# Two attentions of an eight-layer kernel: products in four pieces, maxima split on GpSimd, zero rows by DMA

## The chip, the cores and the metric

The kernel runs on one core of a Trainium2 chip. A core has TensorE (PE, matrix products into PSUM), VectorE (DVE), ScalarE (ACT), GpSimd (POOL, which reaches SBUF only) and SyncE (SP, which here issues nearly all DMAs). Each engine runs its own instructions in order and waits on semaphores for the others. The metric is the time of one execution in microseconds on the device, the median of several runs. PE's clock has two levels, 1.2 and 2.4 GHz; the profile gives the granted clock as a share of the higher one.

## What is computed

The reference is a chain of eight layers on x of 8 x 512 x 128 (float32), attention and feed-forward in turn. The change touches layers 0 and 2 of it, the two multi-head attentions with 16 heads of 8 dimensions each. In the first, two query heads share one of 8 key heads and there is no mask:

```python
scores = jnp.einsum('bsnd,btnd->bnst', q4, k4) * scale
probs = jax.nn.softmax(scores, axis=-1)
a_dot = jnp.einsum('bnst,btnd->bsnd', probs, v4)
```

In the second there are 16 key heads and a causal mask:

```python
scores = jnp.einsum('bhqd,bhkd->bhqk', q, k) / jnp.sqrt(jnp.asarray(d, q.dtype))
mask = jnp.tril(jnp.ones((T, T), dtype=bool))
scores = jnp.where(mask, scores, jnp.asarray(-jnp.inf, q.dtype))
attn = jax.nn.softmax(scores, axis=-1)
return jnp.einsum('bhqk,bhkd->bhqd', attn, v)
```

Between them and after them stand memory terms, mixtures of experts, a two-way state space layer and a last attention, which the change leaves alone.

## The kernel before

`attend` computes one attention for all eight batch rows (chunks, `b`) of 512 tokens. It is called twice, first with `a.causal` false, then with it true; `call` is 0 or 1.

Queries and keys are stacked in SBUF as bf16 parts (72 rows: three parts by three parts of 8 dimensions), `q[k]` and `kk[k]`, two buffers each, k = b mod 2. A score tile (`score_tile`, L771) is a matmul of 128 queries by up to 512 keys over rows 0 to 95 of the stacks, into one of two PSUM banks `sc`; DVE takes the maximum over keys (L911) into `top`. There are four tiles per head. In the causal case tile t covers (t + 1) x 128 keys, and a small matmul with `mask_q` (L774) adds the mask.

When four heads (a group, `g`) are through, `split` (L885 and following) writes the negated maxima as three bf16 parts into `max_part`, a chain of four short DVE instructions on 128x16. PE turns them into rows in bank 0 of `sc` (`turn`, L819), DVE copies the rows to SBUF (`copy_rows`, L901), and GpSimd sends them by two DMAs through DRAM (L745, L748) into rows 96 to 98 of `q[k]`. With these rows the second pass of scores (`scores_of_keys`, L788, keys on the partitions) comes out less its maximum. ScalarE takes its exponential (L856) into `prob`, and `products` (L806) multiplies `prob` by the values `v`, whose ninth column is 1 and gives the denominators. The products are fp32, four heads beside each other in four column tiles of 32, accumulated in `pv`; ScalarE evacuates `pv` (L864) and SP stores it (L672). Afterwards the numerators are divided.

PE's order is written out in `body`. A chunk has eight waves `w` of four rounds `j`. In wave w PE computes the score tiles of heads 2w and 2w + 1 (two tiles a round) and, four waves behind (`BEHIND`), the second pass of one head pair of keys: in wave `wb` for the group wb // 2 and two of the four key tiles (`kp`). The products of the wave before go into rounds 1 and 2:

```python
PV_AT = (1, 2)
...
if j in PV_AT:
    kt = PV_AT.index(j)
```

so that each call multiplies one key tile, four heads at once. The turn comes at the end of round 1 of each even wave. Chunks 0, 1 and the tail are written out; chunks 2 to 7 are three passes of a loop over two chunks on every engine.

`SPAN` gives, for each pair of key tiles, the columns of each: 512 and 512 without a mask, 512 and 384, or 256 and 128, with it. Rows 72 to 127 of `q` must be zero except 96 to 98; rows 64 to 127 of `kk` must be one where they are not loaded. For this GpSimd clears both `q` buffers and both `v` buffers (L717, L718), DVE fills `kk` (L882), and PE begins only when all of it is done. `alone` adds one to a semaphore nobody waits for, as an instruction of its own.

## Time and profile before

| | us |
|---|---|
| median of 3 runs | 4398.98 |
| lowest and highest | 4398.15, 4400.35 |
| the profiled execution | 4399.73 |
| its span in the profile | 4397.6 |
| PE busy | 3343.9 (76%) |
| DVE busy | 2828.6 (64%) |
| ACT busy | 1719.3 (39%) |
| POOL busy | 1054.0 (24%) |
| mean granted clock of PE | 0.873 |

The span is what the trace covers; the time of the run is 2.1 us longer. Busy times are sums over instructions, and the ends of matmuls are modelled, so for PE the starts say more than the durations. In brackets behind a row stands how long its engine had been idle before it, and whose instruction ended that; "issue" means that it waited for nothing that the profile shows. The two attentions stand at 184 to 680 us and at 1490 to 1917 us of the span.

### The profile page before, as it was taken

Reading aid. Unit: us, or ns where it says so; the run is one execution under the profiler, and the core shown is the slowest. Engines: PE = TensorE matmul, PEld = TensorE weight load, DVE = VectorE, ACT = ScalarE, POOL = GpSimd, SP = SyncE. Lnnn points to the kernel's source line nnn. Section 1 sums busy time; section 2 is a strip of 40 time slices with the busy share of each in tenths; the row PEclk is TensorE's granted clock in tenths of the full one; section 3 lists DMA queues with packets and bytes.
Section 4 is the critical chain, followed back from the end, with each engine's and each line's share of the span. In section 5 each row is a group of like instructions: output and inputs, shape, how many; then the busy total and the mean of one; then the engine's idle time right before and its main releaser. Section 6 shows DMA issues by size and latency. Waiting matters only on the chain. (4 is left out here: it accounts for less than half of the span.)

```text
span 4397.6 us, 46982 instructions
## 1 busy us (share of the span) xinstructions
PE 3343.9 (76%) x12317; PEld 1506.2 (34%) x12317; DVE 2828.6 (64%) x4470; ACT 1719.3 (39%) x2599; POOL 1054.0 (24%) x628
## 2 busy tenths in 40 slices
PE   5488886899996488877798666676766668767998
PEld 2122224444443243334444222222222243543443
DVE  6777773333346566655433799999999953355444
ACT  2155553344435244433333554554545413212222
POOL 3200000000002210000000577777777720100000
PEclk7699997899997699988798788888888878878999
DMA  4411101000004522110000333333333310000000
GB/s 135 103 54 50 51 27 29 0 0 0 0 24 123 130 75 76 52 37 0 0 0 20 117 125 124 125 121 119 126 122 119 129 41 0 2 0 0 0 0 19
DMA packets 130753, 250.68 MB, mean 57 GB/s; under 512 B 24661, under 2 KB 100843, under 8 KB 113323
## 3 DMA queue, kind: packets, MB, share of 16 engines
q1 hardware_dynamic: 126506, 247.34, 17.1%
q0 software_dynamic: 4096, 1.59, 0.2%
q8 instruction: 65, 1.06, 0.1%
q14 instruction: 86, 0.70, 0.1%
HBM read 191.98 MB, written 56.89 MB: 57 GB/s over the span
## 5 line engine op out<-in xcount | busy, mean ns | idle before, releaser
L1838 POOL TENSOR_TENSOR a_g<-a_g,a_spread 128x1024 f32<-128x1024 f32 x256 | 660.7, 2587 | 574.5 <-DVE a_g L1796 574.5
L1598 PE MATMUL a_y<-a_g,ident 128*128 128x512 f32 x768 | 451.2, 725 | 362.5 <-POOL a_g L1843 217.5
L911 DVE TENSOR_REDUCE a_top<-a_sc 128x1 f32<-128x512 f32 (+3 forms) x1024 | 567.2, 588 | 238.1 <-PE a_sc L774 118.4
L856 ACT ACTIVATE a_prob<-a_st 128x1024 f32<-128x1024 f32 (+2 forms) x512 | 440.8, 865 | 468.3 <-PE a_st L791 272.2
L1796 DVE TENSOR_TENSOR_SCAN a_g<-a_decay,a_drive 128x512 f32<-128x512 f32 x512 | 596.0, 1204 | 0.0
L455 DVE TENSOR_TENSOR f_s<-f_a,f_spread 128x512 f32<-128x512 f32 x392 | 268.0, 688 | 434.5 <-ACT f_a L440 268.7
L1718 ACT ACTIVATE a_decay<-a_delta,a_capped_a 128x512 f32<-128x512 f32 x512 | 337.2, 712 | 430.4 <-DVE a_capped_a L1768 235.4
L771 PE MATMUL a_sc<-a_k,a_q 96*128 96x512 bf16 (+3 forms) x1024 | 363.0, 360 | 184.3 <-DVE a_top L911 75.1
L422 PE MATMUL f_y<-f_s,f_w 128*128 128x512 f32 x784 | 401.0, 598 | 21.1 <-DVE f_s L455 20.5
L415 PE MATMUL f_hid<-h,f_w 128*128 x784 | 404.9, 601 | 6.2 <-PEq L246 6.2
L1598 PEld LDWEIGHTS a_y<-a_g,ident 128*128 128x128 f32 x768 | 160.6, 224 | 626.4 <-issue 391.2
L1786 DVE TENSOR_TENSOR a_drive<-a_du,a_spread 128x512 f32<-128x512 f32 x512 | 327.6, 686 | 0.3 <-DVE a_g L1796 0.2
L788 PE MATMUL a_st<-a_q,a_k 128*128 128x512 bf16 (+3 forms) x1024 | 282.3, 344 | 16.0 <-issue 10.8
L440 ACT ACTIVATE f_a<-f_hid,f_b,f_scale 128x512 f32<-128x512 f32 x256 | 197.4, 777 | 236.2 <-PE f_hid L415 170.3
L771 PEld LDWEIGHTS a_sc<-a_k,a_q 96*128 96x128 bf16 x1024 | 99.4, 97 | 533.7 <-DVE a_top L911 423.5
L806 PE MATMUL a_pv<-a_prob,a_v 128*32 128x512 f32 (+3 forms) x2048 | 233.4, 529 | 1.7 <-ACT a_prob L856 1.7
L462 DVE TENSOR_TENSOR f_m<-f_a,f_hid 128x512 f32<-128x512 f32 x136 | 93.4, 688 | 212.8 <-ACT f_a L440 212.8
L422 PEld LDWEIGHTS f_y<-f_s,f_w 128*128 128x128 f32 x784 | 145.1, 190 | 223.7 <-issue 160.7
L415 PEld LDWEIGHTS f_hid<-h,f_w 128*128 128x128 f32 x784 | 151.1, 193 | 178.6 <-issue 172.8
L745 POOL DMA_DIRECT2D a_max_rows<-a_max_row x64 | 33.4, 522 | 698.3 <-DVE a_max_row L901 698.3
L440 ACT ACTIVATE f_a<-f_hid 128x512 f32<-128x512 f32 x136 | 81.2, 597 | 264.5 <-PE f_hid L412 263.9
L1843 POOL TENSOR_TENSOR a_g<-a_g 128x1024 f32<-128x1024 f32 x64 | 150.4, 2351 | 5.0
(326 smaller groups left out, 4872.6 us busy)
## 6 DMA issues: line engine op xcount, KB each, us to landing
a_spread<-a_bc_rows SPq DMA_DIRECT2D x128, 1024.0 KB, 4.6
a_q<-a_q_rows SPq DMA_DIRECT2D x64, 288.0 KB
a_pv_rows<-a_pv_sb SPq DMA_DIRECT2D x64, 256.0 KB, 2.1
a_q_rows<-p_qp SPq DMA_DIRECT2D x72, 128.0 KB
a_q_rows<-a1q_qp SPq DMA_DIRECT2D x72, 128.0 KB
a_k_rows<-a1q_kp SPq DMA_DIRECT2D x72, 128.0 KB
a_k<-a_k_rows SPq DMA_DIRECT2D x32, 288.0 KB
a_k_rows<-p_kp SPq DMA_DIRECT2D x72, 64.0 KB
```

The lines of the kernel that those rows point to most:

```text
L415: last = nc.tensor.matmul(hid[:, u % 4, :], unit.w1, h[:, chunk(c)], start=True, stop=True)
L422: nc.tensor.matmul(y[:, :], unit.w2, s[:, u % R, :], start=(u == 0), stop=(u == U - 1 and f.b2 is None)).then_inc(f.used, 1)
L440: nc.scalar.activation(a[:, u % R, :], hid[:, slot, :], f.func, bias=unit.bias if unit.bias is not None else 0.0, scale=unit.scale if unit ...
L771: last = nc.tensor.matmul(sc[:, t % 2, 0:w], q[k][0:MAX_AT, n, t * P:(t + 1) * P], kk[k][0:MAX_AT, n // HK, 0:w], start=True, stop=not a.c ...
L788: last = nc.tensor.matmul(st[:, j % 2, col:col + wide], kk[k][:, n // HK, key:key + P], q[k][:, n, first:first + wide], start=True, stop=n ...
L856: nc.scalar.activation(prob[w % 2][:, j, 0:width(kp)], st[:, j % 2, 0:width(kp)], ACT.Exp, scale=a.scale).then_inc(s.exp_done, 1)
L911: nc.vector.tensor_reduce(top[:, t, n:n + 1], sc[:, t % 2, 0:w], AX.X, ALU.max).then_inc(s.maxed, 1)
L1598: last = nc.tensor.matmul(y[:, k, :], S.ident[:, :], g[:, n % 8, k, :], start=(n == 0), stop=False)
L1718: last = nc.scalar.activation(decay[:, n % 4, k, :], delta[:, d, k, :], ACT.Exp, scale=capped_a[d][:, k, n:n + 1])
L1786: nc.vector.tensor_tensor(drive[:, k, :], du[:, k, :], spread[:, pair % 4, n % 2, :], ALU.mult).then_inc(drive_done, 1)
L1796: nc.vector.tensor_tensor_scan(g[:, n % 8, k, way], decay[:, n % 4, k, way], drive[:, k, way], 0.0, ALU.mult, ALU.add).then_inc(scanned, 1)
L1838: nc.gpsimd.tensor_tensor(g[:, n % 8, :, :], g[:, n % 8, :, :], spread[:, pair % 4, 2 + n % 2:3 + n % 2, :].to_broadcast([P, H2, L]), ALU. ...
```

## The change

`products` gets four pieces in place of two. `PIECES` lists, for each pair of key tiles, tile, column offset and width; piece j goes into round j of the wave. In the causal case the second pair has three pieces of 128 columns, and round 3 stays without. The weights (one value tile) are loaded anew for each piece. Waits that stood at the first key tile now stand at the first piece.

`split` moves from DVE to GpSimd and becomes five instructions: negate, cast, subtract, cast, subtract, with `alone` ahead of the first four and a wait on the chain's semaphore after each. It stands ahead of GpSimd's wait for `max_copied` of the same group and behind the copy of v.

At the start GpSimd clears `q[0]` only; rows 72 to 127 of `q[1]` come as two DMAs of 28 rows from rows 100 to 127 of `q[0]`, and SP waits for them ahead of chunk 1's loads. DVE fills `kk` in four parts per buffer with a count after each. PE no longer waits for all of `v`, `q` and `kk`, only for the loads (which wait for their part) and, in the causal case, for the masks.

```diff
+        if a.causal:
+            PIECES = [[(0, 0, 2 * P), (0, 2 * P, 2 * P), (1, 0, P + P // 2), (1, P + P // 2, P + P // 2)],
+                      [(0, 0, P), (0, P, P), (1, 0, P)]]
+        else:
+            PIECES = [[(0, 0, 2 * P), (0, 2 * P, 2 * P), (1, 0, 2 * P), (1, 2 * P, 2 * P)]] * 2
...
                 if first:
-                    sp.wait_ge(s.q_ready, 8 * call + 4 * k + g + 1)
-                    sp.wait_ge(s.k_ready, 2 * call + k + 1)
+                    if k == 0:
+                        sp.wait_ge(s.q_ready, 4 * call + g + 1)
+                    sp.wait_ge(s.k_ready, 8 * call + 4 * k + g + 1)
...
             load_v(0, 0, first=True)
+            for r in (ROWS, ROWS + 28):
+                sp.dma_start(q[1][r:r + 28, :, :], q[0][P - 28:P, :, :]).then_inc(s.zeroed, 16)
+            sp.wait_ge(s.zeroed, 32 * call + 32)
...
+            for g in range(4):
+                nc.gpsimd.memset(q[0][:, 4 * g:4 * g + 4, :], 0.0).then_inc(s.q_ready, 1)
+            nc.gpsimd.memset(max_part[:, :, :, :], 0.0).then_inc(s.max_step, 1)
             for k in range(2):
-                for g in range(4):
-                    nc.gpsimd.memset(q[k][:, 4 * g:4 * g + 4, :], 0.0).then_inc(s.q_ready, 1)
                 nc.gpsimd.memset(v[k][:, :, :, :], 0.0).then_inc(s.ready, 1)
...
+            def split(b, g):
+                most = top[:, :, 4 * g:4 * g + 4]
+                pool.wait_ge(s.maxed, (nB + b) * 64 + 16 * g + 16 + 2)
+                pool.wait_ge(s.max_turned, 4 * (nB + b) + g)
+                alone(pool, S)
+                chain = Chain(pool, s.max_step, 5 * (4 * (nB + b) + g) + call + 1)
+                chain(nc.gpsimd.tensor_scalar(max_rest[:, :, :], most, -1.0, None, ALU.mult))
+                alone(pool, S)
+                chain(nc.gpsimd.tensor_copy(max_part[:, :, 0, :], max_rest[:, :, :]))
...
+                nc.gpsimd.tensor_tensor(max_part[:, :, 2, :], max_rest[:, :, :], max_part[:, :, 1, :], ALU.subtract
+                                        ).then_inc(s.max_parts, 1)
...
                 for g in range(4):
+                    split(b, g)
                     pool.wait_ge(s.max_copied, 4 * (nB + b) + g + 1)
...
         def _(pe):
-            pe.wait_ge(s.ready, 2 * call + 2)
-            pe.wait_ge(s.q_ready, 8 * call + 8)
-            pe.wait_ge(s.k_ready, 2 * call + 2)
-            pe.wait_ge(s.step, 2 + 6 * call if not a.causal else 2 * call + 6)
+            if a.causal:
+                pe.wait_ge(s.step, 2 * call + 6)
...
-                        if j in PV_AT:
-
-                            kt = PV_AT.index(j)
-                            if w == BEHIND:
-                                if B:
-                                    products(b - 1, 7, k ^ 1, kt)
-                            elif bb is not None:
-                                products(bb, wb - 1, kb, kt)
+                        if w == BEHIND:
+                            if B:
+                                products(b - 1, 7, k ^ 1, j)
+                        elif bb is not None:
+                            products(bb, wb - 1, kb, j)
...
-            def split(b, g):
-                chain = Chain(dve, s.max_step, 4 * (4 * (nB + b) + g) + call + 1)
-                most = top[:, :, 4 * g:4 * g + 4]
-                dve.wait_ge(s.maxed, (nB + b) * 64 + 16 * g + 16 + 2)
...
-                    if n % 4 == 3:
-                        split(b, n // 4)
```

PE's instructions in the last full wave of chunk 1 in the first attention, where `a_st` are the second scores, `a_sc` the score tiles and `a_pv` the products. Before:

```order
L788 MATMUL a_st<-a_q,a_k 128x512 [waits at_exp_done]
L788 MATMUL a_st<-a_q,a_k 128x512
L771 MATMUL a_sc<-a_k,a_q 128x512 [waits at_maxed] x2
L788 MATMUL a_st<-a_q,a_k 128x512 [waits at_exp_done]
L788 MATMUL a_st<-a_q,a_k 128x512
L771 MATMUL a_sc<-a_k,a_q 128x512 [waits at_maxed]
L806 MATMUL a_pv<-a_prob,a_v 32x512 [waits at_evacuated,at_exp_done]
L806 MATMUL a_pv<-a_prob,a_v 32x512 x3
L771 MATMUL a_sc<-a_k,a_q 128x512 [waits at_maxed]
```

And with the change:

```order
L817 MATMUL a_st<-a_q,a_k 128x512 [waits at_exp_done]
L817 MATMUL a_st<-a_q,a_k 128x512
L800 MATMUL a_sc<-a_k,a_q 128x512 [waits at_maxed]
L839 MATMUL a_pv<-a_prob,a_v 32x256 [waits at_evacuated,at_exp_done]
L839 MATMUL a_pv<-a_prob,a_v 32x256 x3
L800 MATMUL a_sc<-a_k,a_q 128x512 [waits at_maxed]
L817 MATMUL a_st<-a_q,a_k 128x512 [waits at_exp_done]
L817 MATMUL a_st<-a_q,a_k 128x512
L800 MATMUL a_sc<-a_k,a_q 128x512 [waits at_maxed]
L839 MATMUL a_pv<-a_prob,a_v 32x256 x4
L800 MATMUL a_sc<-a_k,a_q 128x512 [waits at_maxed]
```

The first burst moved from round 1 to round 0, where it follows the exponentials of the wave before by one round less, and each burst has half the columns.

GpSimd's instructions of one group in the first attention (`a_top` the maxima, `a_max_row` their rows). Before:

```order
L739 COPY a_v<-a_v_in 128x32x8 [waits at_v0]
L745 DMA a_max_rows<-a_max_row 12x512 [waits at_max_copied]
L748 DMA a_q<-a_max_rows 3x2048 [waits at_max_stored]
L745 DMA a_max_rows<-a_max_row 12x512 [waits at_max_copied]
L748 DMA a_q<-a_max_rows 3x2048 [waits at_max_stored]
```

And with the change:

```order
L769 COPY a_v<-a_v_in 128x32x8 [waits at_v0]
L749 TENSOR_SCALAR a_max_rest<-a_top 128x16 [waits at_maxed,at_max_turned]
L751 CAST a_max_part<-a_max_rest 128x4x4 [waits at_max_step]
L753 TENSOR_TENSOR a_max_rest<-a_max_rest,a_max_part 128x16 [waits at_max_step]
L755 CAST a_max_part<-a_max_rest 128x4x4 [waits at_max_step]
L757 TENSOR_TENSOR a_max_part<-a_max_rest,a_max_part 128x4x4 [waits at_max_step]
L776 DMA a_max_rows<-a_max_row 12x512 [waits at_max_copied]
L779 DMA a_q<-a_max_rows 3x2048 [waits at_max_stored]
```

The split came between the copy of v and the group's first DMA; DVE's row of instructions now holds reductions and copies only.

## Rows read from the trace of the kernel before

**Rows 1.** Windows view, first attention: stretch, its length, busy time by engine, PE's clock.

```profile
core 0: us, PE busy (x) PEld busy (x) DVE busy (x) ACT busy (x) POOL busy (x), PEclk, DMA share, GB/s
184.00:680.00 496.00, 422.30 (x2176) 112.36 (x2174) 371.54 (x672) 273.90 (x288) 36.59 (x72) 0.97 0.15 44
```

**Rows 2.** Waits view, 216 to 675 us: us in total, times, longest.

```profile
DVE a_top L911 <- PE a_sc L771: 90.2, 147, 1.7
```

**Rows 3.** Timeline, a round with products, first attention: start, us, instruction, idle before.

```profile
413.09 0.39 PE L771 MATMUL a_sc<-a_k,a_q 96*128 96x512 bf16 x1
...
413.52 1.34 DVE L911 TENSOR_REDUCE a_top<-a_sc 128x1 f32<-128x512 f32 x2 [0.63 <-PE a_sc L771]
413.75 0.38 PE L771 MATMUL a_sc<-a_k,a_q 96*128 96x512 bf16 x1
414.06 1.06 PE L806 MATMUL a_pv<-a_prob,a_v 128*32 128x512 f32 x8
...
415.06 0.39 PE L771 MATMUL a_sc<-a_k,a_q 96*128 96x512 bf16 x1
```

**Rows 4.** Timeline, the split and the turn of a group, first attention.

```profile
402.45 0.17 DVE L890 TENSOR_SCALAR a_max_part<-a_top 128x16 bf16<-128x16 f32 x1
...
403.48 1.89 DVE L911 TENSOR_REDUCE a_top<-a_sc 128x1 f32<-128x512 f32 x3 [0.22 <-DVE a_max_part L894]
...
405.54 0.39 PE L771 MATMUL a_sc<-a_k,a_q 96*128 96x512 bf16 x1
...
407.39 0.38 PE L771 MATMUL a_sc<-a_k,a_q 96*128 96x512 bf16 x1 [0.60 <-DVE a_max_row L901]
```

**Rows 5.** Timeline of GpSimd: the first DMA of groups, in both attentions.

```profile
392.81 0.52 POOL L745 DMA_DIRECT2D a_max_rows<-a_max_row  x1 [12.29 <-DVE a_max_row L901]
...
407.82 0.52 POOL L745 DMA_DIRECT2D a_max_rows<-a_max_row  x1 [12.26 <-DVE a_max_row L901]
...
424.60 0.52 POOL L745 DMA_DIRECT2D a_max_rows<-a_max_row  x1 [14.05 <-DVE a_max_row L901]
...
1666.43 0.52 POOL L745 DMA_DIRECT2D a_max_rows<-a_max_row  x1 [9.70 <-DVE a_max_row L901]
...
1678.87 0.52 POOL L745 DMA_DIRECT2D a_max_rows<-a_max_row  x1 [9.72 <-DVE a_max_row L901]
...
1698.11 0.52 POOL L745 DMA_DIRECT2D a_max_rows<-a_max_row  x1 [16.51 <-DVE a_max_row L901]
```

**Rows 6.** Timeline, causal attention: products of 256 columns and the tile behind them.

```profile
1651.09 0.64 PE L806 MATMUL a_pv<-a_prob,a_v 128*32 128x256 f32 x8
...
1651.66 0.39 PE L771 MATMUL a_sc<-a_k,a_q 96*128 96x512 bf16 x1
```

**Rows 7.** Timeline: short GpSimd instructions elsewhere, and one that waits for DVE.

```profile
8.89 0.29 POOL L98 CAST ident_b<-ident 128x128 bf16<-128x128 f32 x1 [7.28 <-SPq L122]
...
1452.19 0.61 POOL L929 CAST a1q_kp<-a1q_k_rest 128x512 bf16<-128x512 f32 x1 [0.17 <-POOL a1q_k_rest L927]
...
3839.24 2.29 DVE L2059 TENSOR_TENSOR a_attn<-a_e,a_total 128x2048 f32<-128x2048 f32 x1
...
3841.68 1.09 POOL L2073 TENSOR_SCALAR_AFFINE_SELECT a_attn<-a_attn 128x1024 f32<-128x1024 f32 x1 [23.42 <-DVE a_attn L2059]
```

**Rows 8.** Timeline, starts of both attentions; last a DMA: KB each, us to landing.

```profile
167.25 7.04 POOL L717 MEMSET a_q<- 128x2048 bf16 x4 [25.29 <-POOLq L966]
...
183.68 1.01 PE L771 MATMUL a_sc<-a_k,a_q 96*128 96x512 bf16 x2 [22.89 <-POOL a_v L721]
...
1489.71 0.29 POOL L728 TENSOR_SCALAR_AFFINE_SELECT a_mask_k<-a_mask_k 128x128 bf16<-128x128 bf16 x1
...
1490.37 0.27 PE L771 MATMUL a_sc<-a_k,a_q 96*128 96x128 bf16 x1 [39.71 <-POOL a_mask_k L728]
...
1496.47 0.61 POOL L739 COPY a_v<-a_v_in 128x512 f32<-128x512 f32 x1 [6.47 <-DMA a_v_in<-a_v_rows]
...
a_spread<-a_bc_rows SPq DMA_DIRECT2D x128, 1024.0 KB, 4.6
```

**Rows 9.** Timeline of PE at the jump back of the causal loop.

```profile
1691.30 0.61 PE L788 MATMUL a_st<-a_q,a_k 128*128 128x512 bf16 x1 [5.36 <-issue]
```

More of the change, by code:

```diff
@@ L540 @@
 MASKED = -1e30
-PV_AT = (1, 2)
 BEHIND = 4
@@ L569, in attention_semaphores @@
     s.k_ready = sem("at_k_ready")
+    s.zeroed = sem("at_zeroed")
     s.v_ready = sem("at_v_ready")
@@ L729, in _ @@
                                         base=0, pattern=[[1, P]], channel_multiplier=-1).then_inc(s.step, 1)
+            def split(b, g):
[7 more added lines that the diff above has]
+                chain(nc.gpsimd.tensor_copy(max_part[:, :, 0, :], max_rest[:, :, :]))
+                alone(pool, S)
+                chain(nc.gpsimd.tensor_tensor(max_rest[:, :, :], max_rest[:, :, :], max_part[:, :, 0, :], ALU.subtract))
+                alone(pool, S)
+                chain(nc.gpsimd.tensor_copy(max_part[:, :, 1, :], max_rest[:, :, :]))
+                alone(pool, S)
+                nc.gpsimd.tensor_tensor(max_part[:, :, 2, :], max_rest[:, :, :], max_part[:, :, 1, :], ALU.subtract
+                                        ).then_inc(s.max_parts, 1)
+                pool.sem_inc(s.max_step, 1)
             def body(b, A, B, k):
@@ L793, in scores_of_keys, with products @@
                 last.then_inc(s.st_done, 1)
-            def products(bb, w, k, kt):
+            def products(bb, w, k, piece):
                 g, kp = w // 2, w % 2
-                if kt == 0:
-                    pe.wait_ge(s.exp_done, (nB + bb) * 32 + 4 * w + 4 + 2)
-                if kp == 0 and kt == 0:
-                    pe.wait_ge(s.evacuated, (nB + bb) * 4 + g + 1)
-                if w == 0 and kt == 0:
-                    pe.wait_ge(s.v_ready, nB + bb + 1)
-                col, first, wide = SPAN[kp][kt]
+                pieces = PIECES[kp]
+                if piece >= len(pieces):
+                    return
+                kt, off, wide = pieces[piece]
+                if piece == 0:
+                    pe.wait_ge(s.exp_done, (nB + bb) * 32 + 4 * w + 4 + 2)
+                    if kp == 0:
+                        pe.wait_ge(s.evacuated, (nB + bb) * 4 + g + 1)
+                    if w == 0:
+                        pe.wait_ge(s.v_ready, nB + bb + 1)
+                col, first = SPAN[kp][kt][0] + off, SPAN[kp][kt][1] + off
                 for j in range(4):
-                    last = nc.tensor.matmul(pv[32 * j:32 * j + 32, g % 2, first:L],
+                    last = nc.tensor.matmul(pv[32 * j:32 * j + 32, g % 2, first:first + wide],
                                                 v[k][:, 2 * kp + kt, (4 * g + j) // HK, :],
-                                                prob[w % 2][:, j, col:col + wide], start=(kp == 0 and kt == 0),
+                                                prob[w % 2][:, j, col:col + wide], start=(kp == 0 and piece == 0),
                                                 stop=(kp == 1 and kt == 1), tile_position=(0, 32 * j),
                                                 skip_group_check=True)
-                if kt == 1:
+                if piece == len(pieces) - 1:
                     last.then_inc(s.pv_done, 1)
@@ L880, in _ @@
             for k in range(2):
-                nc.vector.memset(kk[k][64:P, :, :], 1.0).then_inc(s.k_ready, 1)
-            nc.vector.memset(max_part[:, :, :, :], 0.0).then_inc(s.max_step, 1)
-            dve.wait_ge(s.max_step, 4 * 4 * nB + call + 1)
-            def split(b, g):
-                chain = Chain(dve, s.max_step, 4 * (4 * (nB + b) + g) + call + 1)
-                most = top[:, :, 4 * g:4 * g + 4]
-                dve.wait_ge(s.maxed, (nB + b) * 64 + 16 * g + 16 + 2)
-                chain(nc.vector.tensor_scalar(max_part[:, :, 0, :], most, -1.0, None, ALU.mult))
-                chain(nc.vector.scalar_tensor_tensor(out=max_rest[:, :, :], in0=most, scalar=-1.0,
-                                                     in1=max_part[:, :, 0, :], op0=ALU.mult, op1=ALU.subtract))
-                chain(nc.vector.tensor_copy(max_part[:, :, 1, :], max_rest[:, :, :]))
-                chain(nc.vector.tensor_tensor(max_part[:, :, 2, :], max_rest[:, :, :], max_part[:, :, 1, :], ALU.subtract))
-                dve.sem_inc(s.max_parts, 1)
+                for g in range(4):
+                    n = KVH // 4
+                    nc.vector.memset(kk[k][64:P, n * g:n * g + n, :], 1.0).then_inc(s.k_ready, 1)
             def copy_rows(b, g):
```

1 line of the change is left out of this document (added).

## The prediction

> **What bounds the kernel now.** The change touches the two attentions alone, some 496 and 427 us of the span. I read the windows view first: in 184 to 680 us TensorE (PE) is busy 422 of 496 us, VectorE (DVE) 372 and ScalarE 274, at a granted clock of 0.97, so no engine alone is the bound [rows 1]. The waits view says who holds whom: in the first attention DVE waits 90 us for a score tile of PE [rows 2]. The timeline shows why. A wave has four rounds; in a round PE issues two `a_st` matmuls, a score tile, perhaps four fp32 products, and a second score tile, and DVE reduces both tiles. In [rows 3] read the starts: tile 413.09, tile 413.75 (with the two `a_st` between them), products 414.06, next tile 415.06. So `a_st` and tile take 0.66, the step from tile to products 0.31 and the products 1.00: a round with products lasts 1.97 us, while DVE needs 1.34 for its two reductions and had stood 0.63 before them. Rounds 1 and 2 of each wave are such rounds; 0 and 3 have none and run at DVE's pace. Twice a wave the pace changes hands.
>
> Once per group of four heads (two waves) two more things come [rows 4]. DVE splits the maxima: from 402.45 to its next reduction at 403.48, 1.03 us in which no score bank is freed. And PE turns them: after the tile of 405.54 comes the turn, DVE copies its result, and PE's next tile starts only at 407.39, 1.85 us from tile to tile where 0.66 would do. So 1.19 us go to the turn. A group lasts 15.0 us in the first attention (392.81 to 407.82) and 12.4 in the second, causal one (1666.43 to 1678.87) [rows 5].
>
> **Products in four pieces.** Non-causal pieces have 256 columns instead of 512. The trace has such a burst, a causal one: 0.57 from its start to PE's next tile (1651.09 to 1651.66) [rows 6], against 1.00 for 512 [rows 3]. Through both points, 128 columns cost 0.36 and 192 cost 0.46, and each burst 0.1 for the switch ahead of it (0.31 less the tile's own 0.21). PE does 8 x 0.67 instead of 4 x 1.10 a group, 1.0 us more. But every round becomes equal: 0.66 + 0.31 + 0.57 = 1.54 us. DVE's pair takes 1.34, so PE sets the pace and DVE is just covered. Alone the edit is worth little: a wave before is 2 x 1.97 + 2 x 1.34 = 6.6, four rounds of 1.54 are 6.2. From below it is worth nothing or less, if a burst's fixed part is larger; from above 0.63 per burst, were PE never late. I take the sum of rounds, since its burst is a row.
>
> **The split leaves DVE.** 1.03 us per group goes. What is late next is PE: the group becomes 8 x 1.54 + 1.19 = 13.5 us against 15.0. ScalarE, busy for 55% of the time, has room.
>
> For the causal attention I scale by columns (0.66 for 1536, so 0.43 for 1000): `a_st` with its masks 0.48 or 0.27 a round, four tiles 0.80 a head. A group is then 3.0 (`a_st`) + 3.2 (tiles) + 2.46 (two pieces of 256, two of 192, each with 0.1) + 1.38 (three of 128) + 1.19 (turn) = 11.25. That is a floor, since DVE's reductions differ in length there; I add 0.15 for hand-overs: 11.4 against 12.45, a gain of 1.05.
>
> **What GpSimd's chain costs.** It is five instructions on 128x16, each waiting for the last. No row shows this size. A cast of 128 columns takes 0.29 and one of 512 takes 0.61 [rows 7], 0.83 ns a column, so 16 columns would take 0.2; from below 0.1, from above 0.29. Between two dependent ones, with the `alone` between them, 0.17 passes (the cast's idle time); from DVE's end to GpSimd's start 0.15 (3839.24 + 2.29 to 3841.68) [rows 7]; from GpSimd's end to PE up to 0.37 (1489.71 + 0.29 to 1490.37) [rows 8]. Sum: 0.15 + 5 x 0.2 + 4 x 0.17 + 0.2 to 0.37 = 2.0 to 2.2; upper end 2.7, lower 1.5.
>
> When is it due? Count from the start of a group's last tile. DVE's reduction starts 0.43 later (413.09 to 413.52) and takes some 0.67: it ends at 1.1. PE could start the turn two rounds on, at 0.23 + 2 x 1.54 = 3.3; but DVE's copy waits for the last tile's reduction until 3.08 + 1.1 = 4.2 anyway, so with 0.6 for the turn and its hand-over a start by 3.6 costs nothing. The window is 2.5 us. In the causal attention the two rounds are 1.24 and 1.44 and the window is 2.1. Inside it four score tiles hide the chain; beyond it each microsecond is one of PE and with it of all. Behind GpSimd's new waits queue its two DMAs of each group and the copy of v. GpSimd sits idle 12.26 of 15.0 us ahead of the first DMA [rows 5], so the group before is done in time. Price: 0 in the first attention, 0.1 per group in the second, 3 us; with 2.7 it is 0.2 and 0.6 per group, 25 us.
>
> The Trainium skill (GPSIMD Engine Reference, Performance versus the Vector engine) has elementwise work about twice as slow there as on VectorE. By it five such ops would take 0.35 each, the chain 2.8 us, and the sum would come out some 25 us higher. It measured long tiles; no row here has a short one on both engines.
>
> **The start.** Before, PE waits for eight memsets of q and both of v: the block's first four memsets start at 167.25 and take 7.04, PE's first tile is at 183.68 [rows 8]. After, PE needs only the stack of group 0: one memset of q (1.76), an eighth of DVE's ones, and two loads. Loads of 1024 KB land in 4.6 us [rows 8]; these have 432 KB, so I take 2 to 5. PE starts about 174.5, 9 us earlier. In the causal one PE still waits for the masks, from which four memsets of q are gone and a small one has come: 7.04 less some 0.4, 6.6. The v copy now stands ahead of the first split. It came at 1496.47, having waited for its load [rows 8]; the loads now begin 5 us earlier, which gives 1491, with the split due about 1494: covered by 3 us. If loads are slower, that start gains 3 only. The zero rows (two DMAs of 448 KB) queue behind v and ahead of chunk 1's loads, which have 40 us: nothing.
>
> **PE's loop.** Chunks 2 to 7 are three passes of a loop over two chunks. At the causal loop's jump back PE stands 5.36 us (to 1691.30) on "issue" [rows 9], and the group takes 19.2 us (1678.87 to 1698.11) instead of 12.4, twice. The first attention's jump costs 424.60 - 407.82 - 15.0 = 1.8 [rows 5], and 0.4 at the second. The bodies differ in length: with a weight load for each matmul and two passes for fp32, some 1300 PE instructions against 1820. The pieces add 128 fp32 matmuls to the first body: 1815, the causal body's length before. So I expect that stall there: 2 x 6.8 - 2.2 = 11 us lost; from below 0, if length is not the cause. Causal: longer still, stall as before.
>
> The Trainium skill (Runtime: NRT & Kernel Launch, Instruction fetch mechanics) says that a taken branch to a page no longer held costs a fetch, and gives TensorE room for 2048 instructions. By that figure 1815 fits and nothing is lost here; but a body of 1820 stalls in this trace, so I go by the row.
>
> **The sum**, against the profiled execution's 4399.7 us (0.7 over the median): first attention 28 groups x 1.47 = 41, its first three groups, mostly without products, 3 for the split, less 11 at the jumps: 33. Second: 28 x 1.05 + 3 - 3 = 29. Starts 9 + 6.6 = 15.6. The ends of the stages, where no score tiles are left, 0 +- 1. Together 78: 4322 us.
>
> **Rivals.**
> No new stall at the jump. For it: only two lengths are seen, a limit between 1300 and 1820 is an assumption. It gives 4311.
> GpSimd's chain is late. For it: short GpSimd instructions are unseen, and register work stands between them in the loop. At 2.7 to 3.0 us, 4347 to 4367.
> Slower than before: the same chain, longer. Past the windows 64 groups pay 64 us for each microsecond; the 78 are used up at about 3.5 us, 0.5 per instruction. At 4 us it is 32 x 1.5 + 32 x 1.9 = 109, less the 3 counted: 4428. Against it: 0.29 for 128 columns.
> The pieces don't even out the rounds. If each pays 0.3 more of fixed cost, rounds are 1.84 and a group 15.9; the starts remain: about 4395. Against it: the 256-column burst.
>
> **How the numbers follow.** Forecast 4322: 50%. No stall, 4311: 17%. Late chain: 20%. Dearer pieces: 6%. Slower: 5%. Starts not gained, 4335: 2%. A measurement of this kernel tells about 0.2%, 9 us, from no change. Faster 0.91, same 0.03, slower 0.06. The range holds the first three, with 11 us below 4311 for hand-overs cheaper than taken: 4300 to 4368.
>
> **What would show it.** Products of 256 columns in every round, rounds 1.54 apart, L745 (now L776) 13.5 us apart. Five GpSimd instructions between a group's last reduction and its turn, 2.0 to 2.2 us in all, the turn not waiting for them. PE's first tile 7 us after the block's first memset. At the first attention's two jumps PE idle for 5 us on "issue". I am wrong if the turn waits for GpSimd in most groups, if rounds are over 1.6, or if groups fall below 13 us.

## The result and the profile after

The changed kernel takes 4356.09 us (median of 4 runs, 4352.24 to 4356.87) against 4399.66 for the kernel before in the same comparison (4398.15 to 4403.35): a ratio of 0.9898, 95% interval 0.9881 to 0.9915. It is 43.6 us faster; the forecast was 78. Its profiled execution has a span of 4354.7 us against 4397.6.

The page of the changed kernel, its first part: busy us, share of the span, instructions.

```profile
PE 3362.5 (77%) x13992; PEld 1542.8 (35%) x14109; DVE 2806.6 (64%) x4224; ACT 1723.7 (40%) x2599; POOL 1112.8 (26%) x942
```

PE has 19 us more to do, DVE 22 less, GpSimd 59 more. The totals don't say where 43 us went; a table by stage does. It is cut at instructions that both traces have (the first memset of an attention's block, the memset of `a_pick` behind it, the memset of `f_parts` in each mixture of experts), so each row is a difference of two starts, in us:

| stretch | before | after | difference |
|---|---|---|---|
| first attention | 516.4 | 479.7 | -36.7 |
| from it to the second | 787.5 | 788.5 | +1.0 |
| second attention | 448.6 | 424.8 | -23.8 |
| behind it to the next mixture | 232.7 | 238.9 | +6.2 |
| that mixture, the state space layers, to the mixture behind them | 1467.3 | 1475.3 | +8.0 |
| that mixture and the next attention | 323.3 | 326.0 | +2.7 |
| the rest | 454.5 | 453.6 | -0.9 |

Another 0.6 lies ahead of the first row. The attentions gain 60.5 us, and 17 are given back in stages in which no line is changed.

Now the lines that answer to [rows 3, 4]. The timeline of the changed kernel, first attention, two rounds and the split (the products' row groups two bursts of four):

```profile
390.37 0.39 PE L800 MATMUL a_sc<-a_k,a_q 96*128 96x512 bf16 x1
...
390.79 1.34 DVE L930 TENSOR_REDUCE a_top<-a_sc 128x1 f32<-128x512 f32 x2 [0.20 <-PE a_sc L800]
...
391.03 0.38 PE L800 MATMUL a_sc<-a_k,a_q 96*128 96x512 bf16 x1
...
391.34 0.64 PE L839 MATMUL a_pv<-a_prob,a_v 128*32 128x256 f32 x8
...
391.91 0.39 PE L800 MATMUL a_sc<-a_k,a_q 96*128 96x512 bf16 x1
...
392.33 0.69 DVE L930 TENSOR_REDUCE a_top<-a_sc 128x1 f32<-128x512 f32 x1 [0.20 <-PE a_sc L800]
...
393.26 0.24 POOL L749 TENSOR_SCALAR a_max_rest<-a_top 128x16 f32<-128x16 f32 x1 [5.44 <-DVE a_top L930]
...
394.82 0.22 POOL L757 TENSOR_TENSOR a_max_part<-a_max_rest,a_max_part 128x16 bf16<-128x16 f32 x1 [0.18 <-POOLq L759]
```

Read the starts: 390.37 to 391.91 is a round, 1.54 us; tile 391.03, products 391.34, next tile 391.91, so 0.31 and 0.57. DVE idles 0.20 in each round where it had idled 0.63. From DVE's end (392.33 + 0.69 = 393.02) to the end of GpSimd's chain (395.04) it is 2.02 us.

GpSimd's first DMA of a group stands for the group, as in [rows 5]. The three lines are from the first attention, with its jump back between the second and the third:

```profile
370.23 0.59 POOL L776 DMA_DIRECT2D a_max_rows<-a_max_row  x1 [1.92 <-DVE a_max_row L920]
...
383.74 0.60 POOL L776 DMA_DIRECT2D a_max_rows<-a_max_row  x1 [2.22 <-DVE a_max_row L920]
...
404.52 0.59 POOL L776 DMA_DIRECT2D a_max_rows<-a_max_row  x1 [9.48 <-DVE a_max_row L920]
```

13.5 us, and then 20.8 over the jump. PE's row at the jump shows why:

```profile
397.79 0.63 PE L817 MATMUL a_st<-a_q,a_k 128*128 128x512 bf16 x1 [5.50 <-issue]
```

And the waits of PE in 216 to 650 us (us in total, times, longest):

```profile
PE a_st L817 <- issue: 12.0, 12, 5.5
PE a_sc L852 <- POOL a_max_part L757: 0.7, 1, 0.7
```

Steady groups take 13.52 us in the first attention (15.0 before) and 11.5 to 11.7 in the second (12.4). PE waits for GpSimd's split once, 0.7 us, in all that stretch. In the second attention it waits for it in most groups, for a short time each. The waits of PE in 1467 to 1861 us:

```profile
PE a_sc L852 <- POOL a_max_part L757: 6.1, 24, 1.0
```

So 24 of the 32 turns there come some 0.2 us late. The start is another matter. The timeline of the second attention's start in the changed kernel:

```profile
1436.05 7.04 POOL L726 MEMSET a_q<- 128x2048 bf16 x4 [17.13 <-POOLq L1256]
...
1436.55 1.76 DVE L914 MEMSET a_k<- 64x2048 bf16 x1 [21.34 <-PEq L1256]
...
1451.53 1.76 DVE L914 MEMSET a_k<- 64x2048 bf16 x1 [0.38 <-issue]
1453.33 0.62 DVE L930 TENSOR_REDUCE a_top<-a_sc 128x1 f32<-128x128 f32 x2
...
1453.67 0.50 PE L800 MATMUL a_sc<-a_k,a_q 96*128 96x384 bf16 x1 [4.91 <-DVE a_top L930]
```

PE has its masks and starts at 1448.05, fills both banks, and then waits 4.91 us for DVE, which fills the second key stack until 1453.3. In the kernel before DVE had filled both stacks before PE began at 1490.37 (the second one and the first reduction):

```profile
1481.48 6.88 DVE L882 MEMSET a_k<- 64x8192 bf16 x1 [1.66 <-issue]
...
1490.85 0.67 DVE L911 TENSOR_REDUCE a_top<-a_sc 128x1 f32<-128x128 f32 x2 [2.33 <-PE a_sc L774]
```

And a group later, GpSimd's two transfers of the first rows of maxima and PE's first use of them:

```profile
1467.08 0.61 POOL L776 DMA_DIRECT2D a_max_rows<-a_max_row  x1 [1.95 <-DVE a_max_row L920]
...
1474.53 0.52 POOL L779 DMA_DIRECT2D a_q<-a_max_rows  x1 [6.84 <-DVE a_top L930]
...
1477.02 0.31 PE L820 MATMUL a_st<-a_mask_k,ident_b 128*128 128x128 bf16 x1 [3.41 <-DMA a_q<-a_max_rows]
...
1482.10 0.60 POOL L776 DMA_DIRECT2D a_max_rows<-a_max_row  x1 [5.21 <-DVE a_max_row L920]
```

The first transfer takes some 7 us from issue to landing, where 2 are usual; chunk 1's loads, issued from 1459.73 on behind SP's wait for the zero rows, fill the queue. The DMA view of 1436 to 1486 us, in 40 slices of 1.25 us, has it at some 190 GB/s up to 1475:

```profile
GB/s 0 7 40 240 197 188 193 191 195 243 188 188 188 280 160 157 157 26 0 21 239 181 189 256 191 175 184 179 193 206 89 25 0 0 0 0 0 10 0 10
```

PE's second pass stands 3.41 us for the rows, and the first group takes 15.0 us (1467.08 to 1482.10) instead of 11.9. In the first attention it is the same: PE stands 2.82 us, 16.0 us instead of 13.3.

### The profile page after: what moved, and what is told of

Read it like the earlier page. It is cut to its first block and busy times, and to the rows that moved or that the text cites. A ratio compares the mean times of both kernels' runs of the same rounds, so it can differ in the third digit from the quotient of the medians.

```text
span 4354.7 us, 50885 instructions
## 1 busy us (share of the span) xinstructions
PE 3362.5 (77%) x13992; PEld 1542.8 (35%) x14109; DVE 2806.6 (64%) x4224; ACT 1723.7 (40%) x2599; POOL 1112.8 (26%) x942
## 3 DMA queue, kind: packets, MB, share of 16 engines
q8 instruction: 94, 1.54, 0.2%
## 5 line engine op out<-in xcount | busy, mean ns | idle before, releaser
L1615 PE MATMUL a_y<-a_g,ident 128*128 128x512 f32 x768 | 461.3, 740 | 368.1 <-POOL a_g L1860 218.6
L930 DVE TENSOR_REDUCE a_top<-a_sc 128x1 f32<-128x512 f32 (+3 forms) x1024 | 583.9, 590 | 210.0 <-PE a_sc L803 121.0
L839 PE MATMUL a_pv<-a_prob,a_v 128*32 128x256 f32 (+2 forms) x3840 | 280.5, 365 | 1.9 <-ACT a_prob L886 1.5
L817 PE MATMUL a_st<-a_q,a_k 128*128 128x512 bf16 (+3 forms) x907 | 255.7, 341 | 17.3 <-issue 12.0
L1642 PE MATMUL a_bank<-h,a_taps 128*128 (+4 forms) x256 | 132.6, 638 | 17.6 <-PEq L1544 15.9
```

The source lines that it names most:

```text
L839: last = nc.tensor.matmul(pv[32 * j:32 * j + 32, g % 2, first:first + wide], v[k][:, 2 * kp + kt, (4 * g + j) // HK, :], prob[w % 2][:, j, ...
L930: nc.vector.tensor_reduce(top[:, t, n:n + 1], sc[:, t % 2, 0:w], AX.X, ALU.max).then_inc(s.maxed, 1)
L1615: last = nc.tensor.matmul(y[:, k, :], S.ident[:, :], g[:, n % 8, k, :], start=(n == 0), stop=False)
```

## The experiments

All times below are medians beside runs of the kernel before on the same chip in the same comparison (4401.1 us for e1 to e4, 4402.4 for e5 to e8, 4398.7 for e9 to e11), and stretches are cut as in the table above.

### One part of the change at a time

Three kernels take the kernel before and one part each. The first has `PIECES` and nothing else, the second the split on GpSimd, the third the start.

```diff
 # e1_pieces
-                        if j in PV_AT:
...
-                                products(bb, wb - 1, kb, kt)
+                            products(bb, wb - 1, kb, j)
 # e2_split
-                    if n % 4 == 3:
-                        split(b, n // 4)
...
                 for g in range(4):
+                    split(b, g)
                     pool.wait_ge(s.max_copied, 4 * (nB + b) + g + 1)
```

> The kernel before with the four pieces alone; the split stays on DVE, the start is the old one. My theory (rounds of 1.54 us): a group of the first attention is 8 x 1.54 + 1.03 (split) + 1.19 (turn) = 14.5 us instead of 15.0, one of the second 12.3 instead of 12.45, and at the first attention's two jumps back PE stands some 5.4 us on issue as in the changed kernel. 28 x 0.45 + 28 x 0.15 - 11 = 6 us faster. Rival 1, the pieces carry the gain: a group falls to 13.9 or less, over 30 us faster. Rival 2, the jump's stall comes from something else than the longer body: no stall at the first attention's jumps here, some 17 us faster. Independent of these, a shift of the stages after the attentions by up to 10 us either way if the place of their instructions matters.

> The kernel before with the split alone moved to GpSimd (five instructions); products stay in two pieces. My theory: the 1.03 us that DVE loses per group come off whole, 14.0 us per group in the first attention and 11.5 in the second, 28 x 1.0 + 28 x 0.95 + 3 = 57 us faster, and no new stall at the first attention's jumps. Rival, the split only helps once the rounds are even (PE is the bound in rounds 1 and 2 and takes up DVE's time): groups of 14.6 or more, under 20 us faster.

> The kernel before with the new start alone (zero rows by DMA, fills of the keys in eight parts, PE not waiting for them). The recorded terms: 9 + 6.6 = 15.6 us faster. Rival, read from the changed kernel's trace: DVE's eight fills hold its first reduction (8.4 us earlier in the first attention, only 2.4 in the second), and the first row transfer of each attention comes among chunk 1's loads, so that the first group is 3 to 4 us longer: 8.4 + 2.4 - 3.5 - 3 = 4 us faster.

Measured: pieces 4379.4 (ratio 0.9946, 0.9929 to 0.9962), split 4348.1 (0.9879, 0.9863 to 0.9896), start 4400.7 (1.0000, 0.9990 to 1.0009).

| | group, first | over its jumps | group, second | first attention | second attention |
|---|---|---|---|---|---|
| before | 15.0 | 16.8, 15.4 | 12.4 | 516.4 | 448.6 |
| pieces alone | 14.2 | 20.1, 20.1 | 12.0 | 502.6 | 440.3 |
| split alone | 13.9 | 14.2, 14.2 | 11.75 | 483.3 | 426.8 |
| start alone | 15.0 | 15.5, 15.4 | 12.4 | 510.4 | 448.9 |
| all three | 13.5 | 20.8, 20.8 | 11.55 | 479.7 | 424.8 |

The timelines of GpSimd, split alone (the jump lies between 392.42 and 406.65) and pieces alone (between 400.93 and 421.00):

```profile
392.42 0.60 POOL L766 DMA_DIRECT2D a_max_rows<-a_max_row  x1 [2.27 <-DVE a_max_row L909]
...
406.65 0.59 POOL L766 DMA_DIRECT2D a_max_rows<-a_max_row  x1 [2.59 <-DVE a_max_row L909]
```

```profile
400.93 0.52 POOL L750 DMA_DIRECT2D a_max_rows<-a_max_row  x1 [11.53 <-DVE a_max_row L907]
...
421.00 0.52 POOL L750 DMA_DIRECT2D a_max_rows<-a_max_row  x1 [17.34 <-DVE a_max_row L907]
```

Three things follow. The split is the change: by itself it is worth 53 us, some 8 more than all three together (4348.1 against 4356.1; the two come from different comparisons and the intervals of their ratios overlap, so the sign of the 8 rests on the stretches of the traces). In the attentions it gains 54.9 us against 60.5, 5.6 less, but the stages behind them take only 3 us more where the whole change pays 17 (on which below). The pieces by themselves are worth 21.7 us, more than the 6 expected, mostly since a group falls by 0.75 us and not 0.45. My reading is that DVE's split hides in part behind PE's now even rounds; no run tests it. But the two overlap. With the split gone from DVE, the pieces take off only another 0.4 us of a group in the first attention and 0.2 in the second, while they bring the stall at two jumps: 28 x 0.4 = 11 won and 2 x 6.6 = 13 lost in the first attention. And the new start gains 6.0 us in the first attention and nothing in the second; alone it leaves the kernel's time as it was (4400.7), since the later stages of its trace take 7.5 us more.

### Is it the length of the loop?

The kernel with the split alone has no stall at the first attention's jump. Idle counter instructions of PE bring its loop to the changed kernel's length.

```diff
                         if A:
                             score_tile(b, 2 * w + j // 2, 2 * j % 4 + 1, k)
+                        if not a.causal and not isinstance(b, int):
+                            for _ in range(8):
+                                alone(pe, S)
```

> The kernel before with the split on GpSimd, products in two pieces, and eight idle counter instructions of PE in each round of the first attention's loop: 512 more in a pass of the loop, so that it has the length of the changed kernel's, 1815 by my count against 1303. Theory, length makes the stall at the jump: the group at each jump is 5 to 7 us longer than the others (0.3 without the idle instructions). Rival, what stands in the loop makes it (the fp32 products' weight loads): no more than 1 us at the jumps.

Measured: groups of 17.0 us, and over the jumps 23.0 and 23.3. The timeline at the first jump:

```profile
418.77 0.60 POOL L766 DMA_DIRECT2D a_max_rows<-a_max_row  x1 [3.41 <-DVE a_max_row L912]
...
434.50 1.03 PE L809 MATMUL a_st<-a_q,a_k 128*128 128x512 bf16 x2 [5.53 <-issue]
...
441.74 0.59 POOL L766 DMA_DIRECT2D a_max_rows<-a_max_row  x1 [9.67 <-DVE a_max_row L912]
```

6.0 and 6.3 us at the jumps, 5.53 of the first on "issue": the length of the body makes the stall, whatever stands in it. The idle instructions cost time of their own (4439.6 us in its only run), 3 us a group. Where between some 1300 and 1815 instructions the stall begins was not tried. The Trainium skill (Runtime: NRT & Kernel Launch, Instruction fetch mechanics) gives PE room for 2048 instructions; by my count the stall is there at 1815, and the changed kernel's trace has 1820 rows of PE from one jump to the next, a few matmul records missing. So a body that fits by the page's figure stalls here, and the measurement decides.

The traces also show the code being read. Their DMA views list transfers of instructions as q8 and q14. Where PE's program alone differs (the changed kernel and the next one below, with PE's loop written out), q8's count differs, 94 and 82, and q14's doesn't; where DVE's alone differs (the last run below), q14's does, 76 and 78. So q8 carries PE's code, 16 KB at a time. The DMA view of the changed kernel, 412 to 632 us, which is its loop from the first jump nearly to the end:

```profile
q8 instruction: 16, 0.26, 0.5%
```

In 412 to 640 us the kernel with the split alone has no such transfer, and neither has the kernel before; the one with idle instructions has 15. The short body isn't read again in these passes, the long one is. One q8 transfer lies within the changed kernel's stall (392.3 to 397.8).

The second test takes the jump away. PE's loop is written out in both attentions, the other engines keep theirs.

```diff
-            steps(pe, body)
+            for b in range(NB + 1):
+                body(b, b < NB, b > 0, b % 2)
```

> The changed kernel, PE's loop over chunks 2 to 7 written out in both attentions (other engines keep theirs). Theory, the jump back has to fetch code: no stall at chunks 4 and 6, 2 x 7.3 us in the first attention and 7.1 + 8.2 in the second come off, 30 us faster than the changed kernel, 4326. Rival, fetching is the limit for long straight code too: the stalls come back spread over the groups, group times over 13.6 and 11.6 us, and the gain is under 10 us. The later stages may shift by up to 14 us either way, as the run with the later code put back to its old places showed.

Measured: 4327.6 us (0.9827, 0.9810 to 0.9843). The timeline of GpSimd where the jump had been:

```profile
383.79 0.60 POOL L776 DMA_DIRECT2D a_max_rows<-a_max_row  x1 [2.22 <-DVE a_max_row L921]
...
397.31 0.59 POOL L776 DMA_DIRECT2D a_max_rows<-a_max_row  x1 [2.23 <-DVE a_max_row L921]
```

13.5 us throughout, and 11.5 and 12.7 at the two places of the second attention where 18.7 and 19.8 had been. (The 12.7, and a 12.2 four groups ahead of it, hold waits of PE for the rows of maxima, 1.24 and 0.76 us, and no stall on "issue".) The first attention takes 466.6 us, the second 410.7: 27 us off the two, where 30 were expected. Four more chunks of PE's code in a row in each attention cost nothing that can be seen, though they are read too: q8 has 13 transfers in 412 to 632 us. So reading code doesn't hold PE while it runs straight on, and the jump back does.

With the jump gone, what are the pieces worth? The kernel with PE written out and the better start of the next section, once with four pieces (e7_fill_unroll) and once with two:

> The kernel with the other start and PE's loop written out, products in two pieces as in the kernel before. Theory, with no jump to pay the pieces are worth what the group times say: 13.9 against 13.52 us in the first attention and 11.74 against 11.47 in the second, 31 x 0.38 + 31 x 0.27 = 20 us slower than with four pieces, 4323. Rival, PE's fewer products leave time that the pieces only move: under 5 us slower, 4303 to 4308.

Measured: 4322.2 us (0.9825, 0.9810 to 0.9840) against 4302.7; groups of 13.91 and 11.75 us against 13.52 and 11.47. The 20 us expected are there, in the medians of two comparisons and in the attentions of the traces (20.5 us). So the pieces are worth some 20 us where no jump is paid for. Behind the loop's end most of that was gone: the two new stalls of the first attention took 13.

### The start

DVE fills the first key stack only. ScalarE fills the second from a tile of ones, GpSimd clears the second query stack behind the masks, and the zero rows by DMA and SP's wait for them are gone.

```diff
-            for r in (ROWS, ROWS + 28):
-                sp.dma_start(q[1][r:r + 28, :, :], q[0][P - 28:P, :, :]).then_inc(s.zeroed, 16)
-            sp.wait_ge(s.zeroed, 32 * call + 32)
...
+                nc.gpsimd.memset(q[1][:, 4 * g:4 * g + 4, :], 0.0).then_inc(s.q1_ready, 1)
...
+                nc.scalar.activation(kk[1][64:P, n * g:n * g + n, :],
+                                     S.ones[64:P, 0:n].rearrange("p (n o) -> p n o", o=1).to_broadcast([64, n, L]),
+                                     ACT.Copy).then_inc(s.k1_ready, 1)
```

> The changed kernel with another start: DVE fills only the first key stack, ScalarE the second one, GpSimd clears the second query stack behind the masks, no zero rows by DMA. Theory, DVE's fills hold the start: first reduction 7 us after the block's first memset in the first attention (8.7 in the changed kernel) and 9.5 in the second (17.3), and the first group falls from 16.0 and 15.0 us to 13 and 12 since chunk 1's loads end before the first row transfer: 1.7 + 7.8 + 3 + 3 = 15 us faster in the attentions. Rival, the loads hold it anyway at their 190 GB/s: first reductions within 2 us of the changed kernel's, first groups at 15 to 16 us, under 5 us in all.

Measured: 4327.8 us (0.9834, 0.9818 to 0.9850). The timeline of the second attention's start:

```profile
1430.16 1.76 DVE L917 MEMSET a_k<- 64x2048 bf16 x1 [21.33 <-PEq L1259]
...
1436.58 1.76 DVE L917 MEMSET a_k<- 64x2048 bf16 x1 [0.38 <-issue]
1438.38 0.62 DVE L933 TENSOR_REDUCE a_top<-a_sc 128x1 f32<-128x128 f32 x2
```

The first reduction comes 8.7 us after the block's first memset (1429.67), where it came after 17.3. The attentions take 473.5 and 417.1 us, 6.2 and 7.7 less than in the changed kernel: 14 of the 15 us expected, but not as expected: the first attention's first group is back at 13.2 us; the second's stays at 15.1. (The other half of this kernel's 28 us is in later stages, see the next section.)

Both edits together:

> Both of the last two edits. Theory: they touch different places and add, 45 us off the attentions of the changed kernel, some 4311 us. Rival: an earlier start meets later loads, or the later stages move to worse places, and it is no better than the better of the two.

Measured: 4302.7 us (0.9775, 0.9759 to 0.9792), the attentions 461.0 and 400.0. They add. The second attention's first group is still 14.6 us. The timeline of GpSimd there:

```profile
1442.66 0.61 POOL L775 DMA_DIRECT2D a_max_rows<-a_max_row  x1 [1.97 <-DVE a_max_row L924]
...
1449.59 0.52 POOL L778 DMA_DIRECT2D a_q<-a_max_rows  x1 [6.33 <-DMA a_max_rows<-a_max_row]
```

The waits of PE in 1420 to 1480 us:

```profile
PE a_st L819 <- DMA a_q<-a_max_rows: 2.8, 1, 2.8
```

The last test holds half of chunk 1's loads until the first rows have landed.

```diff
                     if A and not last and g < 3:
+                        if first and g == 1:
+                            sp.wait_ge(s.max_loaded[0], 64 * (nB // 2) + 16)
                         load(b + 1, g + 1, 1 - k, first=first)
```

> The kernel with the other start and PE's loop written out, and chunk 1's last two groups of loads held until the first rows of maxima have landed. Theory, GpSimd waits for its first row transfer, which lies among chunk 1's loads (6.3 us in the second attention), and the second split is queued behind that wait: the transfer comes down to 4 us or less, the second attention's first group from 14.6 us to 12, 3 us faster than without the hold, 4300. Rival, the loads already issued hold it as long: the group stays at 14 to 15 us, no gain; or the next group's transfer meets the held loads instead and pays the same.

Measured: 4300.4 us (0.9775, 0.9761 to 0.9788, five rounds); the first group of the second attention takes 12.0 us, the attention 397.4. The timeline:

```profile
1443.96 0.61 POOL L777 DMA_DIRECT2D a_max_rows<-a_max_row  x1 [1.97 <-DVE a_max_row L926]
1447.24 0.52 POOL L780 DMA_DIRECT2D a_q<-a_max_rows  x1 [2.67 <-DMA a_max_rows<-a_max_row]
...
1450.69 0.31 PE L821 MATMUL a_st<-a_mask_k,ident_b 128*128 128x128 bf16 x1 [0.22 <-issue]
...
1455.96 0.60 POOL L777 DMA_DIRECT2D a_max_rows<-a_max_row  x1 [2.75 <-DVE a_max_row L926]
```

The transfer is down to 2.67 us and PE doesn't wait. That shows the collision. It also corrects my expectation in one point: I had put the lost time down to the second split, queued behind GpSimd's wait. But the kernel with the start alone has the split on DVE and loses as much (its first group is 15.5 us), with 3.67 us of PE on the rows. It is PE's second pass that waits, for the rows themselves. The 2.3 us between the medians of this kernel and the one without the hold are too few to tell, since they come from two comparisons; the 2.5 us of the second attention's stretch are read from the traces. These kernels beat both the one before and the changed one; this last is the fastest measured, 98 us under the kernel before.

### The stages that were not changed

The changed kernel's stage with the state space layers takes 8 us more than before, with the same lines, DVE busy 1231 and 1228 us and PE's clock at 0.83 in both. DVE is the bound there. Its timeline at the same place of a pass, before and after:

```profile
2862.91 1.22 DVE L1796 TENSOR_TENSOR_SCAN a_g<-a_decay,a_drive 128x512 f32<-128x512 f32 x1
2864.12 1.30 DVE L1786 TENSOR_TENSOR a_drive<-a_du,a_spread 128x512 f32<-128x512 f32 x2
2865.32 2.32 DVE L1796 TENSOR_TENSOR_SCAN a_g<-a_decay,a_drive 128x512 f32<-128x512 f32 x2
```

```profile
2815.22 1.21 DVE L1813 TENSOR_TENSOR_SCAN a_g<-a_decay,a_drive 128x512 f32<-128x512 f32 x1
2816.64 1.30 DVE L1803 TENSOR_TENSOR a_drive<-a_du,a_spread 128x512 f32<-128x512 f32 x2 [0.21 <-DVE a_g L1813]
2818.67 2.33 DVE L1813 TENSOR_TENSOR_SCAN a_g<-a_decay,a_drive 128x512 f32<-128x512 f32 x2 [0.72 <-DVE a_drive L1803]
```

From the fifth on, every other pass of the loop has DVE standing for 0.2 and 0.7 us between its own instructions, always here: passes of 70.8 us where they were 69.7, five times. Further 2.5 us are lost in the first pass and 2.4 where another pass takes 69.6 instead of 67.2. No semaphore holds DVE there. What differs is where its code stands: by my count the change takes 220 instructions from DVE's program ahead of this stage (and adds some 430 to GpSimd's). So I put idle counter instructions behind the second attention, where DVE waits 20 us for its data anyway.

```diff
             steps(dve, body)
+            if a.causal:
+                for _ in range(220):
+                    alone(dve, S)
```

> The changed kernel with idle counter instructions behind the second attention (220 on DVE, 80 on GpSimd, 4 on PE), so that the code of the later stages stands at the same places modulo 256 instructions as in the kernel before. Theory, place matters: the stage of the state space layers takes 5 to 10 us less than in the changed kernel (no 1 us hiccup of DVE in its third instruction of a pass), 4346 to 4350 us in all. Rival, place does not matter: those stages keep their times, and the total is 4356 to 4364, since the idle instructions only add.

> The changed kernel with the 220 idle counter instructions of DVE alone behind the second attention. Theory, it is DVE's code whose place matters: the stage with the state space layers falls from 1475 to 1465 us as it did with all three engines put back, and the passes of 70.8 us come back to 69.7. Rival, GpSimd's or PE's place made it: 1475 us as in the changed kernel.

Measured: all three engines (220 on DVE, 80 on GpSimd, 4 on PE) 4344.1 us (0.9865, 0.9848 to 0.9881), DVE alone 4344.9 (0.9873, 0.9858 to 0.9888), both with the attentions 1 to 3 us longer than in the changed kernel.

| | behind the second attention | to the next mixture | longer passes of 70.8 |
|---|---|---|---|
| before | 232.7 | 1467.3 | none |
| changed | 238.9 | 1475.3 | five |
| changed, code of three engines put back | 234.8 | 1465.0 | none |
| changed, DVE's code put back | 233.3 | 1468.2 | none |

The timeline of the last at the same place of a pass:

```profile
2810.66 1.21 DVE L1816 TENSOR_TENSOR_SCAN a_g<-a_decay,a_drive 128x512 f32<-128x512 f32 x1
2812.13 1.30 DVE L1806 TENSOR_TENSOR a_drive<-a_du,a_spread 128x512 f32<-128x512 f32 x2 [0.26 <-DVE a_g L1816]
2813.34 2.32 DVE L1816 TENSOR_TENSOR_SCAN a_g<-a_decay,a_drive 128x512 f32<-128x512 f32 x2
```

Adding 220 instructions that do nothing makes the kernel some 11 us faster by the medians of two comparisons, and the run with all three engines says the same. In the traces these two stretches take 12.7 us less, and the rest, the attentions most of all, some 5 more. The place of DVE's code is shown as the cause of most of what the unchanged stages cost, 12.7 of 17 us.

How it works is in part to be seen in the traces, and it sorts the kernels. Once per pass of DVE's loop (two of the passes above) q14 brings two blocks of 8 KB close together, and a third. The DMA views of 8 us around them, in the changed kernel (2813 to 2821) and in the last one (2808.7 to 2816.7):

```profile
q14 instruction: 3, 0.02, 0.8%
```

```profile
q14 instruction: 2, 0.02, 0.7%
```

In the changed kernel and in the one with PE written out, whose DVE program is the same, the third block starts 2.4 to 2.6 us behind the second; in the eleven other kernels 5.8 to 16 us behind it. Putting DVE's code back alone moved it from 2.4 to 16 us. These two are the kernels with the 70.8 us passes, and no other has them: the kernel with the better start, with 8 instructions of DVE less, has its third block after 6 us, no such pass, and a stage of 1462.5 us. My reading is that in the two DVE runs out of its first block before the second has come. It fits all thirteen traces, but no run moved DVE's code step by step to test it. The first pass's 2.5 us and the 5.6 us behind the second attention stay without a cause.

## Why the prediction was right and where it was wrong

**Right.** The round of 1.54 us and the burst of 0.57; the group of 13.5 us in the first attention (13.52). GpSimd's chain: 2.02 us against 2.0 to 2.2, and on time in the first attention. In the second it was to cost 3 us; PE's turns wait for it 24 times, 6.1 us in all. That is small, but one of the signs of being wrong, that the turn waits for GpSimd in most groups, is met there. The Trainium skill's rule that GpSimd is about half as fast as VectorE (GPSIMD Engine Reference, Performance versus the Vector engine) did not come out for so short a tile: 0.20 to 0.25 us against 0.17 on DVE [rows 4]. PE's first tile in the first attention came at 174.21, forecast 174.5. The stall at the first attention's jumps was forecast at 6.8 us less what those groups had lost already, 11 us in all; measured against a gain of 1.49 per group, the two jumps lost 4.0 + 5.3 + 3.0 = 12.3. Its cause, the length, is shown.

**Inside the range by luck.** The forecast itself was 4322, and 4356 lies in the 4347 to 4367 that the range held for a late chain of GpSimd. That chain was not late by more than the few us above. What filled the room was something else, most of it in stages that the prediction put at no change.

**The sum was 35 us too good.** The start of the first attention came as forecast (9.3 us for 9). The other terms, against the trace:

- Unchanged stages, put at 0: 17.0 lost. This is the largest miss, and the step that failed is one that the working didn't have: the stages outside the attentions were taken to keep their times. Their code moved, and putting DVE's back gave 12.7 us of it back.
- The second attention's start, 6.6: measured 3.0 to the first DMA of a group, 2.4 to DVE's first reduction. I had counted what PE waits for, the masks, and not DVE: before, its two memsets of `kk` (6.9 us each) ended at 1488.4, ahead of PE's start; once PE starts earlier, they are late. "DVE fills `kk`" stood in the description, and what is late next was not asked of it.
- The first three groups of each attention, 3 us gained each: instead 0.9 and 0.7 lost. The step "nothing" for the zero rows failed. They hold chunk 1's loads until these meet the first transfer of rows, and "40 us" looked only at when the loads are needed, not at whom they delay. Without the zero rows the first attention's first group is back at 13.2 us, while the second's stays at 15.1: there the loads meet the transfer without them too, and only the hold parts the two.
- Groups of the first attention: 41 less 11 is 30; measured 27.8 behind the first three.
- Groups of the second attention: 28 x 1.05 less 3 for GpSimd's chain is 26.4; measured 23.1 behind the first three. A group is 11.55 and not 11.4: the floor was 11.25, I added 0.15 for hand-overs and it took 0.3, with PE's short waits for GpSimd's chain among them.
- The ends: 0 expected. The last group is 0.7 to 0.8 us longer in each attention, and the second's tail 0.9 longer, the first's 1.3 shorter.

**Right in the sum, wrong in the share.** The prediction gave the pieces and the split one gain of 1.5 us a group and said that the pieces alone bring little. In fact they bring 0.75 alone and 0.4 behind the split, and the split alone brings 1.1. "Both together" was right to 0.02 us. But then the recorded numbers already held what matters: 28 x 0.4 against 11 us at the jumps is about nothing. Had I priced the split alone, I would have seen that it gives nearly the whole gain of the two in the first attention.

## What to carry to other kernels

When several edits come together, price each one with the others already in place: behind the split the pieces gave 0.4 us a group where they had given 0.75 alone, and in the first attention the stall that they brought at the loop's end took all of it. Look at the length of a loop's body before adding instructions to it, and where a jump back costs 5 us or more, write the loop out: it was worth 27 us here. When an engine may start earlier, list everything that its first partner still does (DVE's fills) and what the earlier transfers now meet. And be ready for some 10 us from code that merely moves, as here; a trace cut by stages tells it from the edit's effect.

## What the runs showed of the hardware

- A loop body of PE of some 1815 instructions stalls 5.5 us on "issue" at the jump back, one of some 1300 doesn't, also where the difference is 512 idle instructions. The long body's code is read again in each pass (16 transfers of 16 KB in 220 us), the short one's isn't (none in 228 us). With the loop written out the code is read as well (13 transfers), without such stalls.
- Unchanged stages move by up to 14 us with the place of their code; 220 idle instructions of DVE, 11 us less in all. The longer passes come in just the two kernels of thirteen in which three blocks of DVE's code are read within 5 us.
- Five dependent GpSimd instructions on 128x16 take 1.8 us: 0.20 to 0.25 each and 0.17 to 0.19 between them.
- Large loads moved some 190 GB/s; a 12 KB transfer issued among them took some 7 us, where 2 are usual; holding half of them brought it from 6.33 to 2.67.
